# Steps and engines of the routing work in a fused attention and expert kernel: logits and counts last in a step, modulation on DVE, scatters spread over more steps

## The reference, cut to what matters

```python
h = _layernorm(x) * (1 + ca) + sa
x = x + ga * attention(h, Wqkv, Wout)          # window: i-127 <= j <= i
h = _layernorm(x) * (1 + cb) + sb
probs = softmax(h @ gate_w.T + gate_b); topk_prob, topk_idx = top_k(probs, 2)
for c in range(2):                             # the place of a token: how many before it chose the expert
    pos = take(cumsum(one_hot(topk_idx[:, c])) - 1, topk_idx[:, c]); keep = pos < 640
    y = y + expert(topk_idx[:, c])(h) * topk_prob[:, c] * keep   # relu(h W1 + b1) W2 + b2
x = x + gb * y
```

## Time and profile before

| what | value |
|---|---|
| median of 3 runs | 1148.85 us (1147.85 to 1151.25) |
| the profiled execution, its own time | 1158.61 us |
| its span, first to last instruction | 1155.9 us |
| mean granted TensorE clock | 0.985 |
| attention (chunks 0 to 7) in the trace | 54.95 to about 692 us |

### The profile page before, as it was taken

The page is one execution under the profiler, slowest core; times in us unless marked ns, Lnnn a source line. Parts: engine busy times, 40 slices in busy tenths (PEclk is TensorE's granted clock), DMA queues, the critical chain, the costliest instruction groups (busy, mean ns, idle before and its releaser), DMA issues.

```text
span 1155.9 us, 29944 instructions
## 1 busy us (share of the span) xinstructions
PE 1065.9 (92%) x11709; PEld 728.6 (63%) x11709; DVE 764.2 (66%) x1743; ACT 664.2 (57%) x1930; POOL 516.0 (45%) x555
## 2 busy tenths in 40 slices
PE   7999998998998999999977875989999999999996
PEld 4466765665665666666655554755776768585865
DVE  5787677666777776766584684756676666577654
ACT  5687576566565576575572852447474554637361
POOL 2244336364464473473563644334343352424342
PEclk9999999999999999999999997989999999999998
DMA  9744011121121021121123024424345353534000
GB/s 310 143 151 144 21 45 27 36 73 27 43 64 27 25 63 28 36 56 23 35 48 123 2 96 106 94 89 73 101 104 144 87 127 113 112 106 82 22 20 10
DMA packets 140180, 87.70 MB, mean 76 GB/s; under 512 B 96756, under 2 KB 130698, under 8 KB 139916
## 3 DMA queue, kind: packets, MB, share of 16 engines
q1 hardware_dynamic: 129292, 64.29, 21.8%
q0 software_dynamic: 10752, 21.54, 6.6%
HBM read 40.02 MB, written 33.79 MB: 64 GB/s over the span
## 4 chain that ended last, share of the span: by engine, by line
PE 75%; DVE 7%; ACT 6%; issue 6%; POOL 4%; DMA 1%; SPq 0%; DVEq 0%; ACTq 0%; another core or an unknown queue 0%; POOLq 0%
PE down L1773 17%; PE up L1759 17%; PE gen L649 12%; PE gen L768 7%; PE gen L663 6%; PE score L686 5%; PE gen L696 4%; ACT prob L1015 3%; PE pv L725 3%; PE pv L716 2%; DVE prob L1234 1%; POOL h L404 1%; POOL h L408 1%; ACT probT_split L1024 1%; DVE xn L1185 1%
## 5 line engine op out<-in xcount | busy, mean ns | idle before, releaser
L1799 ACT ACTIVATE hid<-up,b1T 128x512 f16<-128x512 f32 (+2 forms) x192 | 122.6, 638 | 184.8 <-PE up L1759 183.3
L1563 POOL TENSOR_SCALAR_AFFINE_SELECT probT_split<-probT_split 128x512 f32<-128x512 f32 x128 | 110.2, 861 | 260.4 <-ACT probT_split L1024 255.7
L1759 PE MATMUL up<-xT,w 128*128 128x512 f16 (+2 forms) x1152 | 212.8, 345 | 13.6 <-issue 13.6
L1773 PE MATMUL down<-w,hid 128*128 128x256 f16 x1920 | 215.1, 275 | 3.2 <-DVE hid L1815 3.2
L1773 PEld LDWEIGHTS down<-w,hid 128*128 128x128 f16 x1920 | 189.2, 99 | 28.4 <-DVE hid L1815 3.7
L649 PE MATMUL gen<-hT,big 128*128 128x512 f16 x768 | 187.8, 384 | 11.5 <-DVE logit L1282 6.2
L1015 ACT ACTIVATE prob<-score,negmax 128x128 f32<-128x128 f32 x512 | 180.7, 373 | 3.2 <-DVE negmax L1226 3.2
L1759 PEld LDWEIGHTS up<-xT,w 128*128 128x128 f16 x1152 | 112.7, 98 | 108.4 <-issue 16.8
L1858 POOL DMA_INDIRECT out<-y,tail x80 | 82.5, 1031 | 209.9 <-DVE y L1843 195.9
L1815 DVE TENSOR_TENSOR hid<-hid 128x512 f16<-128x512 f32 (+2 forms) x192 | 115.0, 606 | 91.6 <-ACT hid L1800 65.0
L1222 DVE COPY_PREDICATED score<-above,score 128x512 f32<-128x512 int32 x112 | 77.7, 694 | 98.9 <-PE score L686 98.6
(11 more groups left out here) (161 smaller groups left out, 1607.9 us busy)
## 6 DMA issues: line engine op xcount, KB each, us to landing
big<-in_L_ffn_W SPq DMA_DIRECT2D x14, 1024.0 KB
slot_inputs<-empty_row SPq DMA_DIRECT2D x80, 129.5 KB, 2.6
out<-x SPq DMA_DIRECT2D x7, 512.0 KB
k<-k SPq DMA_DIRECT2D x48, 64.0 KB, 1.9
x<-in_L_attn_x SPq DMA_DIRECT2D x4, 512.0 KB, 4.4
x<-in_L_attn_x SPq DMA_DIRECT2D x2, 1024.0 KB, 14.8
kept<-out,tail POOLq DMA_INDIRECT x80
out<-y,tail POOLq DMA_INDIRECT x80
```

Source lines behind the costliest of these rows:

```text
L1563: pool.affine_select(out=own, in_=whole, pattern=[[0, TILES], [-1, P]], compare_op=ALU.is_gt, fill=zero, base=0, channel_multiplier=1).the ...
L1759: mm = pe.matmul(bank, w1[:, par, kd, a, ft * P:(ft + 1) * P], part_rows(e, n, xT[:, par, b * KD + kd, :]), start=(i == 0), stop=(i == 5))
L1773: mm = pe.matmul(down[n][:, s, :], hid[:, ft, a, t * P:(t + 1) * P], w2[:, par, ft, b, :], start=(i == 0), stop=(i == 3 * FT - 1))
L1799: act.activation(part_rows(e, n, hid[:, ft, 0, :]), bank, ACT.Relu, scale=1 / W_SCALE, bias=bias).then_inc(hid_hi, 1)
```

## The change

- Within a step, logits and counts stand behind the projections, in steps 5 and 9 (before: ahead of them, in 4 and 7). DVE reads their bank, and that of an output tile, before it begins the step's softmax (`take_logits`, `take_counts`, `gate_tile`); the rest follows later (`shift_logits`, `find_places`, `add_tile`). The counts are 5 products instead of 14.
- Scale and shift of the routed rows go from POOL to DVE (steps 16 and 17); pack goes to step 18 behind ACT's evacuations, the low part to POOL's steps 18 and 19 in halves. SP's `turn_routed` stands behind the next chunk's first keys.
- The next chunk's layer norm: statistics in step 12, aggregation in 16, rows normalised in halves at steps 18 and 19, scale in step 4 and shift in step 6 as one 128x1024 operation each (before: eight of 128x256 with a scalar).
- The low part of the attention output stands behind the softmax of its own step, not ahead of that of the next.
- The eight scatters stand in steps 12 to 16 (before 9 to 12); those of chunk 6's rows in steps 6 to 10 of the last chunk, from a buffer of their own.
- A half of the value products is three products per head instead of four: neighbouring query ranges that use the same values are merged. The turn of prob stays behind them, in chunk 6's last step too.
- In the steps with a value projection, it stands ahead of q or k. The weights of the first expert are loaded one half in chunk 6, the other at its end, to other places.

```diff
-            OUT_TILE = {4: 0, 6: 1, 8: 2, 11: 3}
-            SECOND_V = {5: 0, 7: 1, 9: 2, 10: 3}
+            OUT_TILE = {4: 0, 6: 1, 8: 2, 12: 3}
+            SECOND_V = {5: 0, 7: 1, 9: 2, 11: 3}
...
+            ROUTE_AT = {"stats": (7, 13), "rstd": 14, "norm": 14, "scale": 16, "shift": 17, "token": 18, "pack": 18, "low": (18, 19)}
+            CHOOSE_AT = {"logits": 5, "softmax": 6, "exp": 7, "top": 8, "counts": 9, "slots": 10, "places": 11,
+                         "send": {12: (0, 2), 13: (2, 4), 14: (4, 5), 15: (5, 6), 16: (6, 8)}, "sent": 17}
+            LAST_SENDS = {6: (0, 2), 7: (2, 4), 9: (4, 6), 10: (6, 8)}
+            LAST_SENT = 11
...
+            LN_STATS, LN_AGGR, LN_RSTD, LN_NORM = 12, 16, 17, (18, 19)
+            LN_SCALE, LN_SHIFT, LN_PACK, LN_LOW = 4, 6, 8, 9
...
                         if c > 0:
                             keep_keys(c, (6,))
                             store_rows(c - 1)
                             keep_keys(c, (7,))
+                        if c + 1 < LAST:
+                            keep_keys(c + 1, (0, 1))
                         if c > 0:
                             turn_routed(c)
-                        if c + 1 < LAST:
-                            keep_keys(c + 1, (0, 1))
...
+                    def high_keys(c, u, hd, n):
...
+                        first, last = ((0, P), (P + HALF, 3 * P), (3 * P + HALF, 4 * P))[n]
...
                     def chunk(c):
-                        at = ROUTE_AT
+                        at, pick = ROUTE_AT, CHOOSE_AT
                         for i in STEPS:
-                            if i > LO_AT:
-                                attn_low_part(c, i - LO_AT - 1)
+                            if c > 0 and i - 1 in OUT_TILE:
+                                gate_tile(c - 1, OUT_TILE[i - 1])
+                            if c > 1 and i == pick["softmax"]:
+                                take_logits(c - 1)
+                            if c > 1 and i == pick["slots"]:
+                                take_counts(c - 1)
+                            softmax_step(c, i, False)
+                            if i >= LO_AT:
+                                attn_low_part(c, i - LO_AT)
...
+                            if c > 0 and i == at["scale"]:
+                                route_scale(dve, c)
+                            if c > 0 and i == at["shift"]:
+                                route_shift(dve, c)
...
                     def chunk(c):
                         at, pick = ROUTE_AT, CHOOSE_AT
...
-                            if c > 0 and i == at["scale"]:
-                                route_scale(pool, c)
-                            if c > 0 and i == at["shift"]:
-                                route_shift(pool, c)
-                            if c > 0 and i == at["low"]:
-                                route_low(pool, c)
+                            if c > 0 and i in at["low"]:
+                                route_low(pool, c, at["low"].index(i))
...
-                        if c == LAST - 1:
-                            scatter(c, range(TILES))
-                            pool.wait_ge(sent, 16 * TILES * K * c)
```

More of the change, by code:

```diff
@@ L298, in attn_slot @@
                 return (H * c + u) % ATTN_SLOTS
-            ROUTE_AT = {"stats": (8, 13), "rstd": 13, "norm": 14, "scale": 14, "shift": 15, "token": 16, "pack": 16, "low": 16}
-            CHOOSE_AT = {"logits": 4, "softmax": 5, "exp": 5, "top": 6, "counts": 7, "slots": 8, "send": 9, "sent": 13}
-            LAST_AT = {"stats": 4, "rstd": 5, "norm": 5, "scale": 6, "shift": 7, "token": 7, "pack": 8, "low": 8,
+            ROUTE_AT = {"stats": (7, 13), "rstd": 14, "norm": 14, "scale": 16, "shift": 17, "token": 18, "pack": 18, "low": (18, 19)}
[3 more added lines that the diff above has]
+            LAST_SENT = 11
+            LAST_AT = {"stats": 4, "rstd": 5, "norm": 6, "scale": 6, "shift": 7, "token": 7, "pack": 8, "low": 8,
                        "turn": 9, "logits": 10, "softmax": 10, "exp": 11, "top": 11, "counts": 12, "slots": 12, "send": 13}
@@ L720, in low_keys @@
-                    def low_keys(c, u, hd, i, cur):
+                        r, h, a = DH * hd, 2 * j + hd, 2 * hd * 2 * P
+                        first, last = ((0, P), (P + HALF, 3 * P), (3 * P + HALF, 4 * P))[n]
+                        out_at = (0, HALF, P + HALF)[n]
+                        rows = probT_split[:, n_unit % RING].rearrange("p t m q -> p (t m q)")
+                        return pe.matmul(pv[n_unit % 2][r:r + DH, out_at:out_at + last - first], v[HALF:, 2 * part + n, h * DH:(h + 1) * DH],
+                                         rows[HALF:, a + first:a + last], start=(n == 0), stop=False, skip_group_check=True)
@@ L1187, in ln_second @@
-                        op.then_inc(ln_xn, 1)
-                    def ln_shift(cn, half):
-                        dve.wait_ge(ln_xn, cn + 1)
-                        dve.wait_ge(ln_rstd, cn + 1)
-                        for s in range(2 * half, 2 * half + 2):
-                            op = dve.scalar_tensor_tensor(xn[:, s, :], xn[:, s, :], rstd[0][:, 1, s:s + 1],
-                                                          ln_row[:, batch(cn), 0, :], ALU.mult, ALU.add)
-                        op.then_inc(ln_made, 1)
+                        norm_rows(dve, x_at(cn), xn, meanvar[0], rstd[0], ln_rstd, ln_xn, cn + 1, tiles)
@@ L1252, in add_attention, with add_pair @@
                                                  ga, ALU.mult, ALU.mult).then_inc(gen_free[bank], 1)
+                    def add_pair(c, p):
+                        bank, before = group(c, ("out", p))
+                        at_least(dve, x2_ready, TILES * c + 2 * p)
                         dve.wait_ge(gen_free[bank], before + 1)
@@ L1265, in add_tile @@
                                                  ALU.mult, ALU.mult).then_inc(gen_free[bank], 1)
+                    def add_tile(c, t):
+                        bank, before = group(c + 1, ("tile", t))
+                        at_least(dve, x2_ready, TILES * c + t)
                         dve.wait_ge(gen_free[bank], before + 1)
@@ L1274, in route_tokens, with take_logits, shift_logits @@
                                         token_no[:, c * TILES + t0:c * TILES + t0 + nt].unsqueeze(2)).then_inc(token_put, 1)
-                    def route_softmax(r):
+                    def take_logits(r):
+                        c, t0, nt, rows_out = route_round(r)
+                        bank, before = group(*route_group(r, ("logits",)))
+                        logit = logit_all[:, t0:t0 + nt]
+                        dve.wait_ge(gen_full[bank], before + 1)
+                        dve.scalar_tensor_tensor(logit, gen[bank][:, 0:nt * E].rearrange("p (s e) -> p s e", e=E), 1 / W_SCALE,
+                                                 gbB[:].unsqueeze(1).to_broadcast([P, nt, E]), ALU.mult, ALU.add)\
+                           .then_inc(gen_free[bank], 1)
+                    def shift_logits(r):
                         c, t0, nt, rows_out = route_round(r)
```

329 lines of the change are left out of this document (179 added, 150 removed).

## The result

Changed kernel: median 1112.12 us of 4 runs (1111.55 to 1115.21), beside 1148.57 of 4 (1147.85 to 1151.25) for the kernel before. The ratio is 0.9684, 95% interval 0.966 to 0.9708: 3.2% faster, where 1112 was forecast. The profiled executions stand at 1115.21 (span 1113.4) against 1158.61 (span 1155.9): 42.5 us of span, while the medians differ by 36.5. The profile before was taken in an execution 0.9% above its median, the one after 0.3% above, so the trace shows more than the metric.

The account below looks back on a forecast made before the run. PE bounds the attention part, with some 7 us of waits per routed chunk. Terms sum to -37.4 us against 1158.61, 3.2%; taken off the 1148.85 median this gives 1112 us, range 1098 to 1130.

Parts of the forecast that it names:

- logits and counts: Steps 4 and 7 of five routed chunks: moved last, behind projections, they save 1.95 and 0.8 a chunk, -13.8 us.
- the new wait at step 4: PE's value products wait for POOL's selects, queued behind its low part of the routed rows: 0.3 x 6, +1.8 us.
- normalisation in halves: Rows normalised two at a time at steps 18 and 19, low part straight after softmax: 1.0 in chunks 1 to 4, -4.0.
- batch change: Chunk 3: POOL's shift no longer holds DVE's copy_predicated for 2.63 us; -3.5 us.
- scatters: Moved from steps 9 to 12 to 12 to 16: two thirds of 1.8 us lost in steps 10 and 11, -3.0 (0 to -9).
- chunk 0: 3.3 us lost before; new normalise and scale of chunk 2 in step 4; half the loss remains, -1.8 us.
- turns of h2T: Four turns on the SP queue land at about 10.5, logits want them at 10.6; +0.2 x 5 = +1.0 us.
- DVE's price: Each 128x1024 two-input operation moved to DVE takes 1.4 us (1.2 to 3.3), with zero cost on the path.
- Rival B: The lock moves with the work: DVE's operations and POOL's selects block each other, six chunks lose 3 us each; 1130 us, 0.24.
- A: All stalls go: scatters collide with nothing, no new wait, boundary undisturbed, value products win; -55.5, 1094 us, chance 0.13.
- C: Slower: late turns of h2T make PE's logits wait at step 5; at 9 us late per chunk 1160 us, chance 0.05.
- D: No change: the gaps are refilled by ACT, busy 51.5 of 82.5 us; 1149 us, chance 0.02.

Follow-up runs that it names:

- a_unmerged: Changed kernel with four value products per head and half again, in the loops of the kernel before; 1115.65 us, ratio 0.9724.
- a_pack_gap: Changed kernel with both packs on ACT right behind the copy of the turned prob, ahead of the projections' evacuations; 1111.39 us, ratio 0.9693.
- b_logits_first: Kernel before, with DVE reading the logits' bank before adding the output tile's rows, products left in place; 1138.92 us, ratio 0.9933.
- b_no_scatter: Kernel before without the 40 scatters of the rows of chunks 0 to 4 and the waits for their completion; 1147.56 us, ratio 0.9925.
- a_norm_early: Changed kernel with chunk 2's rows normalised ahead of chunk 0 instead of in its step 4; 1116.06 us, ratio 0.9637.
- b_dve_mod: Kernel before with scale and shift of the routed rows on DVE instead of POOL, in their old steps 14 and 15; 1159.5 us, ratio 1.0025.
- a_pool_mod: Changed kernel with scale and shift of the routed rows back on POOL, in the same steps 16 and 17; 1122.63 us, ratio 0.9795.
- a_low_next: Changed kernel with the attention low part back ahead of the next step's softmax; 1154.56 us, ratio 0.9979.
- the repeat: Changed kernel run again unaltered, in the third group of experiments; 1113.61 us, ratio 0.9708.

## Why the prediction was right, and where its terms were not

The total was right and the range held it. The terms were right in part; large errors of opposite sign cancel, and that the total came out within 1 us is luck. Sums over the steps of the two profiled executions, after less before (-42.3 together, by a span of -42.5):

| term of the prediction | forecast | measured |
|---|---|---|
| logits and counts, with the new wait at step 4 | -13.8 + 1.8 | -6.7 |
| step 16, chunks 1 to 5 | -7.8 | -7.8 |
| normalisation in halves, chunks 1 to 4 | -4.0 | -3.1 (step 18; chunk 3's lies in its step 17) |
| batch change | -3.5 | -4.1 |
| scatters (steps 10 to 13, chunks 2 to 6) | -3.0 (0 to -9) | -11.1 |
| chunk 0 | -1.8 | +1.2 |
| chunk 6, steps 15 to 18 | -2.4 | -3.5 |
| boundary of chunks 6 and 7 | -4.9 | -4.8 |
| weight load in chunk 6, turns of h2T | +1.0, +1.0 | 0, 0 |
| merged value products | 0 | -0.1 a chunk (a_unmerged), within the other rows |
| before chunk 0; experts; the rest of chunks 1 and 7 | 0 | +1.2; -4.3; +0.7 |

*Logits and counts* were mis-sized by what came in their place. PE's wait for DVE's logits did go. Step 4, forecast at 6.0 to 6.3, is 7.2, and step 9 holds 0.44 of wait for ACT's copy of the turned prob, which stands behind the pack of step 8. I had priced the new wait at step 4 at 0.3, as POOL's selects late behind its low part. It is 1.0, and what is late is DVE: the step that failed is "the new place of the pack is behind ACT's evacuations, with nothing of the same step behind it". True of the same step; the next step's exponentials are behind it. a_pack_gap shows that POOL's low part is a second cause, which takes over when the pack is early. b_logits_first shows that reading the bank first, without moving the logits, is cheaper: steps 4 and 5 of chunk 5 take 11.7 together, against 12.4 in the changed kernel.

*Scatters* were the other error, outside my own bounds. I took the 1.8 us of steps 10 and 11 as the whole loss and kept two thirds of it. The loss was also in step 13, and all of it went. b_no_scatter shows it to be bound to scatters, b_logits_first that they need not go or move for it to go: 9.9 of the 11.1 us came there from the order of two reads. So no run shows that the new steps of the scatters won anything, and a_norm_early, where steps 13 and 16 are stretched beside scatters, suggests that the loss can return. I had no ground for "two thirds".

*DVE's price*. Forecast 1.4 (1.2 to 3.3) for a 128x1024 operation; measured 1.82, 1.31, 1.29 and 1.23 mean. The cheap end is its own time (1.23 in b_dve_mod); the scale takes up to 2.24, in chunk 5, beside POOL's selects. It is hidden, as forecast. The Trainium skill, page "SBUF — State Buffer", section "Who interferes with whom", says that a vector instruction with two SBUF inputs contends with a GpSimd one that reads SBUF, and that the first to issue blocks the other. The trace of a_pack_gap agrees in the order of starts (POOL at 422.94, DVE's 0.68 operation stretched to 1.48 from 423.13), and that of a_pool_mod too (POOL at 494.53, DVE's stretched to 3.48 from 494.54). In b_dve_mod most of what step 15 lost, 1.23 of 1.85, is DVE's own queue and no contention.

*Rival B* (0.24) was the one to weigh more: its outcome, though mostly not by its lock, is what happens in the old order. What decides against it is the place of the low part, which the prediction priced at 1.0 in four chunks under "normalisation in halves" and which a_low_next prices at 34 us. Without it few of my other terms would have held: the batch change stays gone (chunk 3's step 17 at 4.65), but step 16 of chunks 3 to 5 is back at 5.95 to 6.02, and nearly every step with once-per-chunk work is longer. The prediction named the edit and not its function: it takes the low part, for which PE waits, out from behind everything else that DVE does.

*Chunk 0*. The new work in step 4 costs more than its slack: PE idles 2.14 for the low part in step 6 (it ends at 65.47, and PE is busy again from 65.7). I had kept half the old loss as a gain without tracing who waits. Of the 1.2 lost, 1.6 are clock (below); the repeat has 61.85, a gain of 0.44.

*Rivals A, C, D*. C is out: the logits' group (L844) has an idle time of 0.0 over chunks 1 to 6, so the turns of h2T are never late. D is out with chunk 5 at 77. A's stalls did go where the scatters were and stayed at steps 4 and 9.

*The experts' 4.3 us* is not the change's. In the traces of b_logits_first and b_no_scatter, where the experts are those of the kernel before, that stretch is 4.3 and 4.4 us shorter than in the profile before, too.

## What to carry to other kernels

Put the operation that frees the busiest engine's next bank directly behind the work of its own step, ahead of all once-per-chunk work: then that work can be laid on the same engine for almost nothing. Without it, the one move of work that was tried here gained nothing, and the whole change 0.2%. When a late operation goes "behind everything" in its step, look at the first thing of the next step on that engine. Where a wait stays after its cause is removed, look for a second cause of the same size; only a kernel with both removed, which is missing here, would show that there is no third.

## What the runs showed of the hardware that was not expected

- The same pause can cost twice. In chunk 0's step 6 PE idles 2.14 us in both traces of the changed kernel; in one the granted clock is 1.00 (2.4 GHz) through the step and it takes 5.61, in the other it is 0.50 (1.2 GHz) from 65.7, where the pause ends, to 68.5, and the step takes 7.21, with PE busy 5.07 instead of 3.47. a_pack_gap has 7.17 there at 0.76; four others of the runs have 5.60 to 5.61:

```profile
62.70:69.91 7.21, 5.07 (x52) 3.25 (x51) 6.45 (x14) 3.08 (x11) 2.58 (x4) 0.76 0.47 159
```

```profile
62.51:68.12 5.61, 3.47 (x52) 2.18 (x51) 5.61 (x14) 3.09 (x11) 2.10 (x3) 1.00 0.46 155
```

- Indirect DMAs issued by POOL go with short PE pauses for which the trace names no semaphore, 1.1 us over steps 10 and 11 of the kernel before (chunk 5), and the pauses vanish if the scatters are absent (b_no_scatter) or if the step pattern around them shifts by 1.5 us (b_logits_first).
- A DVE operation of 0.68 us takes 1.48 when it begins 0.19 behind a POOL operation of 1.13 (a_pack_gap), and 3.48 when it begins 0.01 behind one of 2.37 that a select follows (a_pool_mod).
- Where an instruction waits for several things, the releaser that the profile names can be off: in four kernels it named ACT's evacuation once and POOL's selects three times, while PE started 0.31 to 0.32 after the end of DVE's low part each time.
